# Two accumulators in DRAM instead of one for the outputs of the experts, each with its own chain of adding scatters

## The reference, cut to what matters

```
x  = hidden_states                                # (8, 512, 128)
xn = layernorm(x)
out = x + bidirectional_mamba(xn) + moe(xn)

# moe, for each token:
logits     = -|xn - keys|^2 + xn @ rw.T + rb      # 16 experts
topv, topi = top_k(logits, 4);  w = softmax(topv)
moe        = sum over the 4 chosen e of  w_e * (gelu(xn @ w1[e].T + b1[e]) @ w2[e].T + b2[e])
```

## Time and profile before

| | before |
|---|---|
| median of 3 runs | 1144.69 us (1136.71 to 1153.21) |
| the profiled execution's own time | 1141.97 us |
| its span, first to last instruction | 1140.1 us |
| DVE busy | 1042.6 us (91%) |
| ACT busy | 940.7 us (83%) |
| PE busy | 933.3 us (82%) |
| POOL busy | 900.5 us (79%) |
| the 160 adding scatters (L768) on POOL | 252.5 us, 1578 ns each |
| granted TensorE clock, mean | 0.938 of full speed |

### The profile page before, as it was taken

One profiled execution on the slowest core, in us unless ns is written; L12 is line 12 of the kernel. 1 busy time (PEld: TensorE's weight loads), 2 busy tenths in 40 slices (PEclk: granted clock), 3 DMA queues, 4 the chain that ended last, 5 costly groups with the idle time before them and its releaser, 6 DMA issues.

```text
span 1140.1 us, 21850 instructions
## 1 busy us (share of the span) xinstructions
PE 933.3 (82%) x5866; PEld 738.2 (65%) x5866; DVE 1042.6 (91%) x1354; ACT 940.7 (83%) x1732; POOL 900.5 (79%) x545
## 2 busy tenths in 40 slices
PE   4476886754899988999998889899999989898982
PEld 2233332323678777878877677788788778776771
DVE  7878998959999999999999999999999999896991
ACT  4258888775899999999998889999999999887920
POOL 3278778657579979998999799799989989995742
PEclk9789989775899999999999999999999999998995
DMA  9924564486666867687687668677866877764545
GB/s 312 365 102 166 203 220 183 158 327 191 231 177 167 215 196 186 180 233 193 174 218 187 181 175 238 184 184 194 224 188 172 220 202 203 170 158 124 140 111 159
DMA packets 151299, 222.65 MB, mean 195 GB/s; under 512 B 36028, under 2 KB 97756, under 8 KB 146276
## 3 DMA queue, kind: packets, MB, share of 16 engines
q1 hardware_dynamic: 124036, 202.16, 56.0%
q0 software_dynamic: 27136, 19.02, 11.7%
HBM read 159.74 MB, written 65.52 MB: 198 GB/s over the span
## 4 chain that ended last, share of the span: by engine, by line
issue 22%; POOL 17%; DMA 6%; PE 6%; ACT 5%; DVE 3%; SPq 2%; POOLq 0%; DVEq 0%; ACTq 0%
POOL arena L783 9%; POOL acc_d L768 8%; DMA acc_d<-yrows,tags 4%; DVE arena L1479 2%; PE ps L1188 2%; ACT arena L990 2%; DMA tags<-slots_d 1%; PE ps L1159 1%; DVE ps L1467 1%; PE ps L1220 1%; ACT arena L930 1%; ACT arena L911 1%; ACT arena L958 1%; PE ps L1180 1%; DMA arena<-acc_d 0%
## 5 line engine op out<-in xcount | busy, mean ns | idle before, releaser
L1479 DVE TENSOR_TENSOR_SCAN arena<-arena,ps 128x512 f32<-128x512 f32 x512 | 597.3, 1201 | 1.1 <-issue 1.0
L783 POOL TENSOR_TENSOR arena<-arena 128x1024 f32<-128x1024 f32 x237 | 510.1, 2455 | 68.2 <-DVE arena L1479 67.4
L990 ACT ACTIVATE arena<-delta,a_neg 128x511 f32<-128x511 f32 x512 | 340.5, 726 | 6.0 <-DVE arena L1426 3.3
L768 POOL DMA_INDIRECT acc_d<-yrows,tags x160 | 252.5, 1578 | 61.1 <-issue 36.4
L1159 PE MATMUL ps<-ident,arena 128*128 128x128 f32 x2048 | 274.1, 278 | 7.5 <-POOL arena L783 5.1
L1467 DVE TENSOR_TENSOR ps<-du,ps 128x512 f32<-128x512 f32 x352 | 232.3, 675 | 23.0 <-PE ps L1223 20.4
L1159 PEld LDWEIGHTS ps<-ident,arena 128*128 128x128 f32 x2048 | 236.4, 144 | 20.7 <-POOL arena L783 5.6
L750 POOL DMA_INDIRECT slots_d<-arena,pos x128 | 161.0, 1258 | 47.3 <-issue 44.4
L1188 PE MATMUL ps<-w,arena 128*128 128x128 f32 x1248 | 174.7, 283 | 3.5 <-ACT arena L958 2.4
L1180 PE MATMUL ps<-rowsT,w 128*128 128x256 f32 x640 | 155.8, 387 | 11.6 <-ACT arena L941 7.6
L1188 PEld LDWEIGHTS ps<-w,arena 128*128 128x128 f32 x1248 | 154.2, 192 | 14.0 <-issue 4.5
(11 more groups left out here) (147 smaller groups left out, 913.5 us busy)
## 6 DMA issues: line engine op xcount, KB each, us to landing
arena<-c_d SPq DMA_DIRECT2D x128, 512.0 KB, 4.2
w<-w_dram SPq DMA_DIRECT2D x80, 258.0 KB
w<-w_dram SPq DMA_DIRECT2D x80, 256.0 KB
rows<-slots_d SPq DMA_DIRECT2D x80, 130.0 KB
slots_d<-delta SPq DMA_DIRECT2D x5, 2015.0 KB, 19.2
delta_d<-arena SPq DMA_DIRECT2D x8, 1024.0 KB, 3.9
du_d<-delta SPq DMA_DIRECT2D x8, 1024.0 KB, 6.2
delta<-delta_d SPq DMA_DIRECT2D x8, 1024.0 KB, 7.4
```

What stands on the lines that cost most here:

```text
L768: pool.indirect_dma_start(acc_d, bass.IndirectOffsetOnAxis(ap=tags[:, j, a, 0:1].bitcast(I32), axis=0), yrows[:, j % W_RING, a, :], None, ...
L783: nc.gpsimd.tensor_tensor(state[:, q % H_RING], state[:, q % H_RING], c_rows[:, r % C_RING], ALU.mult).then_inc(s["prod_done"], 1)
L990: nc.scalar.activation(decay[:, q % DA_RING, j, lo:lo + L - 1], delta[:, par, dh, lo:lo + L - 1], ACT.Exp, scale=a_neg[:, dh, 2 * g + j:2 ...
L1479: nc.vector.tensor_tensor_scan(state[:, q % H_RING, j, way], decay[:, q % DA_RING, j, way], b_ps[:, ROW[q, j], j, way], 0.0, ALU.mult, ALU ...
```

## The change

`acc_d` becomes a list of two accumulators. `acc_d[0]` is filled with `x` as before and takes the even tiles; `acc_d[1]` is filled with zeros and takes the odd ones. The zeros come from `du[:, 0]`, a buffer of 8 KB per partition that the preparation doesn't use: POOL sets it to zero at its start, and SP stores it with four DMAs (4.13 MB in all) after the second `store_gate`. SP waits for all the fills before it loads `du[:, 0]` for the first sequence. `sums_landed` waits for the scatters of the earlier tiles of the same parity only. At the end SP waits for the even tiles, reads `acc_d[0]` in eight DMAs, waits for the odd tiles, and reads `acc_d[1]` in eight more. DVE adds the scan branch to the first seven sums of `acc_d[0]`, then the eight of `acc_d[1]`, and last the scan branch of the last sequence from PSUM.

```
-        acc_d = dram("acc_d", (UNUSED + TOK, D))
+        acc_d = [dram(f"acc{i}_d", (UNUSED + TOK, D)) for i in range(W_RING)]
...
+ZERO_ROWS = DH * L // D
+ZERO_ACC = [(at, min(ZERO_ROWS, (UNUSED + TOK - at) // P)) for at in range(0, UNUSED + TOK, P * ZERO_ROWS)]
+ACC_DMAS = 1 + BATCH + len(ZERO_ACC)
...
# SP, read_ahead
             sp.wait_ge(s["slots_zeroed"], 16 * ZERO_DMAS)
+            sp.wait_ge(s["acc_filled"], 16 * ACC_DMAS)
...
# SP, preparation
             store_gate(1)
+            sp.wait_ge(s["zero_acc"], 1)
+            for at, n in ZERO_ACC:
+                sp.dma_start(acc_d[1][at:at + P * n].rearrange("(p r) d -> p (r d)", p=P),
+                             du[:, 0, :, :].rearrange("p q l -> p (q l)")[:, 0:n * D]).then_inc(s["acc_filled"], 16)
...
# SP, end
             for i in range(W_RING):
                 sp.wait_ge(y_out[i], 16 * SH * (NTILE // W_RING))
+                for b in range(BATCH):
+                    sp.dma_start(acc[i][:, b, :], acc_d[i][UNUSED + L * b:UNUSED + L * (b + 1)].rearrange("(p t) d -> p (t d)", p=P))\
+                        .then_inc(acc_in[i][b], 16)
             for b in range(BATCH):
-                sp.dma_start(acc[:, b, :], acc_d[UNUSED + L * b:UNUSED + L * (b + 1)].rearrange("(p t) d -> p (t d)", p=P))\
-                    .then_inc(acc_in[b], 16)
-            for b in range(BATCH):
-                sp.wait_ge(s["acc_ready"], b + 1)
+                sp.wait_ge(s["acc_ready"], BATCH + b)
...
# POOL
+            nc.gpsimd.memset(du[:, 0, :, :], 0.0).then_inc(s["zero_acc"], 1)
...
-            pool.wait_ge(s["acc_filled"], 16 + 16 * BATCH)
+            pool.wait_ge(s["acc_filled"], 16 * ACC_DMAS)
...
             def sums_landed(b, before, j):
                 half = MPB // W_RING * (b - before)
-                for i in range(W_RING):
-                    wait(pool, y_out[i], 16 * SH * (half + (j + W_RING - 1 - i) // W_RING))
-                    pool.sem_inc(s["pool_step"], 1)
+                wait(pool, y_out[j % W_RING], 16 * SH * (half + j // W_RING))
+                pool.sem_inc(s["pool_step"], 1)
...
-                    pool.indirect_dma_start(acc_d, ...
+                    pool.indirect_dma_start(acc_d[j % W_RING], ...
...
# DVE, end
             dve.wait_ge(s["mixed_in"], 32)
+            for b in range(BATCH - 1):
+                dve.wait_ge(acc_in[0][b], 16)
+                nc.vector.tensor_tensor(acc[0][:, b, :], acc[0][:, b, :], scanned[b * 2 // BATCH][:, b % (BATCH // 2), :],
+                                        ALU.add).then_inc(s["acc_ready"], 1)
             for b in range(BATCH):
-                dve.wait_ge(acc_in[b], 16)
+                dve.wait_ge(acc_in[1][b], 16)
                 if b < BATCH - 1:
-                    scan_sum = scanned[b * 2 // BATCH][:, b % (BATCH // 2), :]
+                    dve.wait_ge(s["acc_ready"], b + 1)
+                    nc.vector.tensor_tensor(acc[0][:, b, :], acc[0][:, b, :], acc[1][:, b, :], ALU.add).then_inc(s["acc_ready"], 1)
                 else:
-                    bank_written(dve, s, BATCH, "O", 0, 1, True)
-                    scan_sum = m_ps[1]
-                nc.vector.tensor_tensor(acc[:, b, :], acc[:, b, :], scan_sum, ALU.add).then_inc(s["acc_ready"], 1)
+                    nc.vector.tensor_tensor(acc[0][:, b, :], acc[0][:, b, :], acc[1][:, b, :], ALU.add).then_inc(s["acc_last"], 1)
+            bank_written(dve, s, BATCH, "O", 0, 1, True)
+            dve.wait_ge(s["acc_last"], 1)
+            nc.vector.tensor_tensor(acc[0][:, BATCH - 1, :], acc[0][:, BATCH - 1, :], m_ps[1], ALU.add).then_inc(s["acc_ready"], 1)
```

More of the change, by code:

```diff
@@ L369, in build_kernel @@
         late = delta[:, 0].rearrange("p q l -> p (q l)").rearrange("p (t f s) -> p t f s", t=2, f=FC)
-        hidden = carve(GROUP * FC * S).rearrange("p (t f s) -> p t f s", t=GROUP, f=FC)
+        hidden_all = carve(GROUP * FC * S)
+        hidden = hidden_all.rearrange("p (t f s) -> p t f s", t=GROUP, f=FC)
         hidden = [hidden[:, t] for t in range(GROUP)] + [late[:, t] for t in range(2)]
-        acc = decay.rearrange("p r j l -> p (r j l)")[:, 0:BATCH * TPB * D].rearrange("p (b n) -> p b n", b=BATCH)
+        acc = [t[:, 0:BATCH * TPB * D].rearrange("p (b n) -> p b n", b=BATCH)
+               for t in (decay.rearrange("p r j l -> p (r j l)"), hidden_all)]
         scanned = [t[:, 0, :, :].rearrange("p q l -> p (q l)").rearrange("p (b n) -> p b n", b=BATCH // 2) for t in (delta, du)]
@@ L451, in build_kernel @@
         m_ps = [ps[:, 6, :], ps[:, 7, :]]
-        names = """consts_in route_in wts_in a_exp zero_v slots_zeroed var_ready std_ready xn_ready xnT_ps xnT_ready
+        names = """consts_in route_in wts_in a_exp zero_v zero_acc slots_zeroed var_ready std_ready xn_ready xnT_ps xnT_ready
             kw_ready bias_ready behind_ready experts_ready xn_act_ready shift_ready score_ps score_ready sel_ready logit_ps keys_ps chosen_ready rank_ps pos_ready gdiff_ready gexp_ready
@@ L462, in build_kernel @@
             b2_in b2_split b2_out turn_ps turned scaled
-            mixed_out mixed_in sp_step pool_step acc_ready out_done"""
+            mixed_out mixed_in sp_step pool_step acc_ready acc_last out_done"""
         s = {n: sem(n) for n in names.split()}
@@ L470, in build_kernel @@
         y_out = [sem(f"y_out{i}") for i in range(W_RING)]
-        acc_in = [sem(f"acc_in{b}") for b in range(BATCH)]
+        acc_in = [[sem(f"acc{i}_in{b}") for b in range(BATCH)] for i in range(W_RING)]
         block = ctx.enter_context(nc.Block())
@@ L510, in _ @@
                              delta[:, :, :, :].rearrange("p a q l -> p (a q l)")[:, 0:n * RW]).then_inc(s["slots_zeroed"], 16)
-            sp.dma_start(acc_d[0:UNUSED], x_in[0:UNUSED]).then_inc(s["acc_filled"], 16)
+            sp.dma_start(acc_d[0][0:UNUSED], x_in[0:UNUSED]).then_inc(s["acc_filled"], 16)
             for b in range(BATCH):
-                sp.dma_start(acc_d[UNUSED + L * b:UNUSED + L * (b + 1)].rearrange("(p t) d -> p t d", p=P),
+                sp.dma_start(acc_d[0][UNUSED + L * b:UNUSED + L * (b + 1)].rearrange("(p t) d -> p t d", p=P),
                              x_in[L * b:L * (b + 1)].rearrange("(t p) d -> p t d", p=P)).then_inc(s["acc_filled"], 16)
@@ L692, in _ @@
                 sp.wait_ge(y_out[i], 16 * SH * (NTILE // W_RING))
+                for b in range(BATCH):
+                    sp.dma_start(acc[i][:, b, :], acc_d[i][UNUSED + L * b:UNUSED + L * (b + 1)].rearrange("(p t) d -> p (t d)", p=P))\
+                        .then_inc(acc_in[i][b], 16)
             for b in range(BATCH):
-                sp.dma_start(acc[:, b, :], acc_d[UNUSED + L * b:UNUSED + L * (b + 1)].rearrange("(p t) d -> p (t d)", p=P))\
-                    .then_inc(acc_in[b], 16)
-            for b in range(BATCH):
-                sp.wait_ge(s["acc_ready"], b + 1)
+                sp.wait_ge(s["acc_ready"], BATCH + b)
                 sp.dma_start(out[L * b:L * (b + 1)].rearrange("(t p) d -> p t d", p=P),
-                             acc[:, b, :].rearrange("p (t d) -> p t d", t=TPB)).then_inc(s["out_done"], 16)
+                             acc[0][:, b, :].rearrange("p (t d) -> p t d", t=TPB)).then_inc(s["out_done"], 16)
             sp.wait_ge(s["out_done"], 16 * BATCH)
@@ L767, in send @@
                 for a in range(SH):
-                    pool.indirect_dma_start(acc_d, bass.IndirectOffsetOnAxis(ap=tags[:, j, a, 0:1].bitcast(I32), axis=0),
+                    pool.indirect_dma_start(acc_d[j % W_RING], bass.IndirectOffsetOnAxis(ap=tags[:, j, a, 0:1].bitcast(I32), axis=0),
                                             yrows[:, j % W_RING, a, :], None, compute_op=ALU.add).then_inc(y_out[j % W_RING], 16)
```

## The result

Over 19 runs of each kernel the median went from 1139.23 us (1134.59 to 1153.21) to 1133.42 us (1128.73 to 1141.6). The ratio is 0.9946 with a 95% interval from 0.9924 to 0.9968: 6.2 us less, between 3.6 and 8.7. The forecast was 1136, the range 1126 to 1148.

A forecast was written before the change was run, and what follows sets the result against it. DVE was taken to bound the loop and the late scatter chain the end. Reads 16.3 us sooner, less 7.1 for eight more reads and 0.8 for an add, gain 8.4: 1144.69 becomes 1136, range 1126 to 1148.

The forecast's parts named there:

- The bound: DVE paces the loop (592.74 of 600 us busy); the end is set by the chain of scatters, some 16 us late.
- The start of the reads: At the end, SP starts on the even sum when the scans end, 1108.5 instead of 1124.76: 16.3 us earlier.
- The last tiles: Each tile waits for tile j-2; tile 7 sent at 1096.5, landed 1105.7; tile 9 sent at 1106.4, landed 1111.8.
- The sixteen reads: At the end, eight more reads follow the first eight without a gap, 0.89 us each: 7.1 us added.
- the reads hold back the last scatter: Rival: tile 9's landing is seen only after the eight even reads; gain 6.6 us, time 1138; chance 0.13.
- the prediction's own signs: Right: sixteen reads in one run from about 1108; wrong: odd reads several us apart, tile 9 landing past 1120, or ACT waiting.
- The adds and stores: At the end, DVE adds 16 times; only one new add follows the last read, 0.8 us; stores follow as before.
- Rival E: At the end, reads take 0.61 us each before the stores start: gain 12.5 us, time 1132; chance 0.08.
- The fill and POOL's program: Preparation's zeros and memset fit under existing waits, 0 us; POOL's fewer waits in the loop, taken as 0, bounds 0 and 1.5.
- Rival C: Scatters of two tiles in flight take twice as long; chain still ends near 1124.7; +0.8 us, 1145.5; chance 0.13.
- D: Rival: in the preparation, C's store waits behind the zeros until ACT wants the buffer; 16 us slower, 1160; chance 0.06.
- The forecast's level: The 8.4 us gain was taken off the three-run median of 1144.69 us, giving 1136.3.

The follow-up runs named there:

- scan sums early: Changed kernel with SP's seven scan sums read during the last sequence: ratio 0.9887 to the kernel before, 0.9886 on chip 2; last scan to end 20.4 us.
- the two kernels with one accumulator: Kernel before with only SP's scan-sum read moved earlier, to q == 20 or q == 17: ratios 1.0038 and 0.9983; last scan to end 33.5 and 28.0 us.

## Why the prediction was right, point by point

**The bound** was read rightly: putting the old order back takes all of the gain away, and DVE's loop did not move.

**The start of the reads** was to come 16.3 us sooner: before it lay 16.30 us behind the last scan, after 0.03.

**The last tiles.** Tile 7's landing was drawn out by SP's reads of the scan sums, as forecast (7.46 us for 7.31). The rest slipped by one small step, met twice on the way to tile 9: from the end of ACT's scaling to POOL's start of the tile there were 0.87 us (for tile 9 from 1105.51 + 0.63 to 1107.01), of which I had counted 0.07 (for tile 7 from 1095.8 + 0.63 to 1096.5). So tile 7 started 11.1 us before the end of the last scan, not 12.0, and tile 9 was sent 0.2 us before it instead of 2.1.

**The sixteen reads** were the step that failed. The sum had "the other eight follow without a gap", eight more at 0.89 us each: 16.05 us from first issue to last landing. It was 17.3, and by another way. The odd reads started 1115.37 - 1107.26 = 8.1 us behind the even ones, and each eight took about as long as the eight of before: 9.1 us (1107.26 to 1116.39) and 9.2 (1115.37 to 1124.58), for 8.91. Without the gap sixteen took 14.0 (scan sums early) and 13.9 (both parities awaited), so there the second eight added some 5 us, not 7.1. The pace in one run would have been 2.0 us better than the forecast, and the gap that I had left to a rival took 3.3.

**That rival, the reads hold back the last scatter,** was given 0.13, and its mechanism is what happened, if not to the letter: the scatter landed at 1115.36, before the eighth even read (1116.39) and not behind all eight. By the prediction's own signs it was this rival's case: the odd reads stood apart from the even ones, and only a landing without reads beside it took 3.26 us. I had argued that the scatter goes out "before most of those reads". On the forecast's times some three reads would have been out when POOL had finished with it; sent 1.9 us later against the scans, it had some seven of the eight in front of it (1108.86 + 1.55 = 1110.41, at one read in 0.46 us). On the scale of before, whose last scan ended 1.23 us later, the last read landed at 1124.58 + 1.23 = 1125.8, nearer to the rival's 1126.4 than to the forecast's 1124.6.

**The adds and stores.** From the last landing to the end of the last add it was 1.50 us, 0.72 before: the added one cost 0.78, and I had counted 0.8. The stores then took 4.9 us instead of 5.7, which no case had; why is open. Together these make the forecast's 23.2 into 23.8: 16.27 - (17.32 - 8.91) - 0.78 + 0.79 = 7.9 us of gain, within rounding of the 7.8 measured. So the end stretch came nearer to the forecast's gain of 8.4 than to the rival's 6.6 only by the 0.8 us of the stores. That is luck: the start of the reads and the adds were right, the reads without a gap were not. The 6.2 us of the runs, with their interval of 3.6 to 8.7, fit both.

**Rival E,** faster reads, has its pace in part (sixteen in one run took 14.0 us), but the changed kernel did not get it. Its time of 1132 came close for another reason, the base of the forecast (below).

**The fill and POOL's program** cost nothing, as said. ACT does not wait for C, and the memset of 1.80 us stands in front of a load's wait that is 13.48 us now; POOL's cast behind it came at 19.84 instead of 19.40, and nothing later in the preparation shows it.

**Rival C** (the change doesn't shorten the chain) and **D** (the fill delays the preparation) fell: tile 9 has landed by 1115.4 and not by 1124.7, and the fill of twice the size shows how much room there was.

**The forecast's level.** A gain of 8.4 us was set against a median of three runs, 1144.69. Nineteen runs give 1139.23 for the same kernel, so the 2.9 us between 1136.3 and 1133.4 are 5.5 us of a base that was too high, less 2.6 us by which the gain came out smaller than 8.4. Two misses cancel in part.

What stays open: of the 7.8 us of the profiled end stretch, runs show 6.2 with an interval of 3.6 to 8.7. The two agree, and more can't be said with this spread.

## What to carry to other kernels

A chain of dependent scatters is late by its landings, and a second target makes two chains of it, for the price of one more pass over the result; take what each landing costs from the trace, and ask what else is on the DMA engines in that moment. A transfer that is started sooner can hold up the small one that everything waits for: the early even reads here bought 1.2 us net at most, not the 3 to 4 that their start promised. Move large reads that have long been possible away from the end, to a place where no landing is on the chain, before adding memory.

## What the runs showed of the hardware that I had not expected

**A small scatter beside large reads.** The second scatter of a tile landed 3.2 to 3.5 us after its issue when SP's queue moved next to nothing meanwhile (3.18, 3.25, 3.26, 3.28, 3.36; 4.04 once, when POOL took 2.39 us and not 1.55 to send it), a little later beside loads of some 0.3 MB (3.67 and 3.92), and 5.84 to 7.52 us when SP moved 1 to 2 MB beside it (7.31 before; 7.46 and 6.50 after; 7.29 and 7.44; 6.64; 7.52 and 6.42 with the fill of twice the size; 7.29 where SP waited for both parities; 7.33 and 6.40; 7.40 and 5.84). The two kinds come from different queues. Where the scatter had fewer reads in front of it, some four or five in place of seven, it landed sooner (5.84). The Trainium skill, "DMA: Bandwidth & Descriptors", section "Queues, rings and completion order", says that a semaphore's increment lands only after every earlier write on the same DMA engine, whichever queue they came by. These landings do not contradict it, but they do not need it: the scatter's own data was late. In the changed kernel no packet of POOL's queue moved between 1112.25 and 1113.1, and those of tile 9's second scatter moved from 1113.1 to 1115.1, 4.2 to 6.2 us after its issue. Where SP waited for both parities they moved from 1112.85 to 1113.85, 2.0 to 3.0 us after it. The landing came within 0.4 us of the last packet in both. It is the same in the row of 7.31 that the prediction puts beside the rule: no packet of POOL's queue moved in the 2.6 us from its issue, 1099.43, to 1102.0. Why the engines came to that data so late is open.

**Eight reads and sixteen.** Eight reads of 256 KB took 8.7 to 8.9 us from the first issue to the last landing (before, and the two kernels with one accumulator), sixteen in one run 13.9 to 14.05 (three profiles). Within the first five reads of each there was a pause of 1.2 to 2.0 us between two landings, and from the ninth on one landed every 0.67 us: the 0.89 of the forecast is the mean of a start, and the kernel with two runs of eight pays for the start twice. The stores are not the cause. Before, their data began to move only at 1132.2, 1.5 us before the last landing, and where SP waited for both parities it issued stores from 1124.09 on while the reads kept landing every 0.67 us until 1128.07.

**The spread of the runs** goes with the mean granted TensorE clock of the execution. Of the changed kernel on one chip, an execution at 0.926 took 1138.07 us and one at 0.948 took 1121.96; over the runs of the kernel before, on three chips, time and mean clock correlate by -0.60 to -0.73, some 3 to 4 us for 0.01 of the clock. DVE paces the loop, so I had not looked there; which of the two moves the other no run here shows. It means that here 6 us want some twenty runs, or one well-chosen stretch of the trace.
